# Graph layer on one core: 51 single-row fetch steps go from ScalarE's DMA queue to GpSimd's gathers

## The reference, cut to what matters

```
h    = relu(layernorm(x))
w    = edge_weight / segment_sum(edge_weight, dst)[dst]
feat = relu(h @ W_pool + b_pool)
neigh  = segment_max(feat[src] * w, dst)
rst  = h @ W1_self + neigh @ W1_neigh + b1;  h1 = relu(rst / |rst|)
neigh2 = segment_sum(h1[src] * w, dst) / deg
out  = x + relu(h1 @ W2_self + neigh2 @ W2_neigh + b2)
```

## Time and profile before

| | us |
|---|---|
| median of 3 runs | 5000.1 |
| lowest and highest | 4995.1, 5009.1 |
| the profiled execution | 5002.4 |
| its span in the trace | 5000.6 |

### The profile page before, as it was taken

The page is one execution under the profiler, slowest core; times in us unless marked ns, Lnnn a source line. Parts: engine busy times, 40 slices in busy tenths (PEclk is TensorE's granted clock), DMA queues, the critical chain, the costliest instruction groups (busy, mean ns, idle before and its releaser), DMA issues.

```text
span 5000.6 us, 64383 instructions
## 1 busy us (share of the span) xinstructions
PE 3637.2 (73%) x15531; PEld 1723.2 (34%) x15531; DVE 3011.2 (60%) x6735; ACT 1430.3 (29%) x4018; POOL 2954.1 (59%) x3127
## 2 busy tenths in 40 slices
PE   1345663588888888887557888888888888888864
PEld 1334442233333333333323333333333333333323
DVE  1656665566666666666446656666666666666654
ACT  1434443222222222222443222222222222222220
POOL 6366656655565555565656555655555555655655
PEclk5756565699999999998768999998999999999977
DMA  4244332322223222322433233232323333333236
GB/s 135 82 144 134 99 97 96 101 91 92 87 88 97 87 86 90 94 88 93 128 92 93 91 97 99 93 106 89 96 89 101 96 95 101 96 93 103 91 112 175
DMA packets 283743, 502.39 MB, mean 100 GB/s; under 512 B 64740, under 2 KB 200164, under 8 KB 258532
## 3 DMA queue, kind: packets, MB, share of 16 engines
q1 hardware_dynamic: 170756, 290.79, 16.8%
q0 software_dynamic: 99552, 204.13, 15.5%
q10 hardware_dynamic: 13056, 3.37, 0.3%
HBM read 260.17 MB, written 237.86 MB: 100 GB/s over the span
## 4 chain that ended last, share of the span: by engine, by line
ACTq 37%; issue 21%; PE 19%; ACT 6%; DVE 6%; another core or an unknown queue 6%; DVEq 3%; DMA 1%; POOL 1%; SPq 0%; POOLq 0%
ACTq L704 29%; ACTq L719 7%; PE pM L1250 3%; ACT pT L741 3%; PE pM L1248 3%; ACT pM L741 2%; PE pM L1249 2%; PE pC L1250 2%; PE pC L1248 2%; PE pC L1249 2%; DVEq L952 2%; DVE S L958 1%; DVE CP L1036 1%; DVE S L955 1%
## 5 line engine op out<-in xcount | busy, mean ns | idle before, releaser
L609 POOL DMA_INDIRECT G<-h_tab,SRC x1437 | 1359.0, 946 | 954.8 <-issue 429.5
L609 POOL DMA_INDIRECT G<-feat_tab,SRC x1390 | 1320.9, 950 | 943.6 <-issue 391.8
L1036 DVE TENSOR_SCALAR CP<-pH,kcode 128x1024 bf16<-128x1024 bf16 x1225 | 912.6, 745 | 352.1 <-PE pC L1250 115.7
L741 ACT ACTIVATE pM<-G,EW 128x128 f32<-128x128 f32 x1440 | 530.8, 371 | 1621.2 <-issue 1482.6
L741 ACT ACTIVATE pT<-G,EW 128x128 f32<-128x128 f32 x1387 | 509.0, 370 | 1302.1 <-issue 1139.7
L1036 DVE TENSOR_SCALAR U<-pR,kcode 128x1024 bf16<-128x1024 bf16 x735 | 547.3, 745 | 94.3 <-PE pM L1250 46.8
L1248 PE MATMUL pC<-CP,A 128*128 128x512 bf16 x1274 | 506.7, 398 | 125.0 <-DVE CP L1036 82.5
L1248 PE MATMUL pM<-CP,A 128*128 128x512 bf16 x1176 | 467.2, 397 | 129.0 <-DVE CP L1036 87.0
L1249 PE MATMUL pC<-CP,A 128*128 128x512 bf16 x1274 | 505.3, 397 | 18.7 <-issue 17.0
L955 DVE SCALAR_TENSOR_TENSOR S<-S,C,pM 128x128 f32<-128x128 f32 x780 | 271.2, 348 | 372.2 <-ACT pM L741 233.5
L1222 PE MATMUL pH<-CP 128*128 128x98 bf16 x1563 | 301.2, 359 | 266.6 <-DVE CP L974 133.7
(11 more groups left out here) (203 smaller groups left out, 4193.8 us busy)
## 6 DMA issues: line engine op xcount, KB each, us to landing
scan<-S SPq DMA_DIRECT2D x97, 1032.0 KB
scan<-S SPq DMA_DIRECT2D x97, 1024.0 KB
GA<-h_tab ACTq DMA_DIRECT2D x3328, 0.5 KB
GA<-feat_tab ACTq DMA_DIRECT2D x3200, 0.5 KB
G<-h_tab,SRC POOLq DMA_INDIRECT x1437
G<-feat_tab,SRC POOLq DMA_INDIRECT x1390
U<-own_tab SPq DMA_DIRECT2D x48, 256.0 KB
CP<-codes SPq DMA_DIRECT2D x25, 256.0 KB
```

Of the source, the lines that this page charges most:

```text
L609: pool.indirect_dma_start(out=dst, out_offset=None, in_=table, in_offset=bass.IndirectOffsetOnAxis(ap=idx, axis=0)).then_inc(s, 16)
L741: act.activation(scaled(t), v, ACT.Copy, scale=EW[:, t:t + 1]).then_inc(s_mul, 1)
L1036: dve.tensor_scalar(HOT[phase][:, k % NHOT, :], sources(phase).bitcast(BF16), kcode[:, j:j + 1], None, ALU.is_equal).then_inc(s_o2, 1)
```

## The change

ScalarE fetches no rows any more. The 51 steps of `ROWA` join `GORD`, in the order of their steps, so GpSimd makes 1415 gathers in phase 0 and 1463 in phase 1, through the same ring of 16 buffers. The buffers `GA`, the offsets `IX`, their load, their shift on VectorE and the waits for them go. All else is as before.

```diff
-ROWA = [(phase, row_step(phase, m)) for phase in range(2) for m in range((25, 26)[phase])]
-FETCHED = set(ROWA)
-GORD = [(0, t) for t in SEQ if (0, t) not in PAT and (0, t) not in FETCHED] + \
-    [(1, t) for t in range(TS) if (1, t) not in PAT and (1, t) not in FETCHED]
+GORD = [(0, t) for t in SEQ if (0, t) not in PAT] + [(1, t) for t in range(TS) if (1, t) not in PAT]
...
-        GA = sb("GA", [P, NGS, D])
-        IX = sb("IX", [P, P], I32)
...
-                    sp.dma_start(IX[:, :], srcr).then_inc(s_ixl, 16)
...
-            def fetch_row(to, phase, reg, s):
-                at = act.snap(reg, donate=True)
-                act.dma_start(to.bitcast(U8), flat[phase][bass.ds(at, 4 * D)].rearrange("(a d) -> a d", a=1))\
-                    .then_inc(s, 16)
...
-                    if p == 0 and k >= NGS:
-                        ph, before = ROWA[k - NGS]
-                        act.wait_ge(s_mul, ph * TS + before + 1)
-                    if p % RL == 0:
-                        ahead[:] = [act.alloc_register(f"arow{k}_{p + r}") for r in range(RL)]
-                        act.load(ahead, IX[k:k + 1, p:p + RL])
-                    fetch_row(GA[p:p + 1, k % NGS, :], phase, ahead[p % RL], s_arow[k % NGS])
...
-                fetch_rows(phase, t)
...
-                elif (phase, t) in AAT:
-                    k = AAT[phase, t]
-                    act.wait_ge(s_arow[k % NGS], 16 * P * (k // NGS + 1))
-                    v = GA[:, k % NGS, :]
...
-                    dve.wait_ge(s_ixl, 16)
-                    dve.tensor_scalar(IX[:, :], IX[:, :], 9, None, ALU.logical_shift_left).then_inc(s_ix, 1)
```

More of the change, by code:

```diff
@@ L123 @@
 TWO = 0x40000000
-U8 = mybir.dt.uint8
 def tiles_of(g):
@@ L165, in own_store_block, with build @@
     return (OWN_FIRST + OWN_EACH * (g + 1)) // T + 1
-def build(nc, x, src, srcq, srcr, dstx, ew, w_pool, b_pool, w1s, w1n, b1, w2s, w2n, b2, out):
+def build(nc, x, src, srcq, dstx, ew, w_pool, b_pool, w1s, w1n, b1, w2s, w2n, b2, out):
     feat = nc.dram_tensor("feat_tab", (NP, D), F32).ap()
@@ L328, in build @@
         s_sst = [sem(f"s_sst{i}") for i in range(NS)]
-        s_arow = [sem(f"s_arow{i}") for i in range(NGS)]
-        s_ixl = sem("s_ixl")
-        s_ix = sem("s_ix")
         s_oh = sem("s_oh")
@@ L460, in raw_arrived @@
                 eng.wait_ge(s_x[max(i for i in range(len(LOADS)) if sum(LOADS[:i]) <= g)], 16)
-        flat = [tab.rearrange("n d -> (n d)").bitcast(U8) for tab in (feat, htab)]
         block = ctx.enter_context(nc.Block())
@@ L697, in _ @@
                     act.activation(C[:, :], M[:, :], ACT.Identity, scale=-NEG, bias=neg[:, 0:1]).then_inc(s_c, 1)
-            ahead = []
-            def fetch_row(to, phase, reg, s):
-                at = act.snap(reg, donate=True)
-                act.dma_start(to.bitcast(U8), flat[phase][bass.ds(at, 4 * D)].rearrange("(a d) -> a d", a=1))\
-                    .then_inc(s, 16)
[L707 to L713, removed]
-                    if p == 0 and k >= NGS:
-                        ph, before = ROWA[k - NGS]
-                        act.wait_ge(s_mul, ph * TS + before + 1)
-                    if p % RL == 0:
-                        ahead[:] = [act.alloc_register(f"arow{k}_{p + r}") for r in range(RL)]
-                        act.load(ahead, IX[k:k + 1, p:p + RL])
-                    fetch_row(GA[p:p + 1, k % NGS, :], phase, ahead[p % RL], s_arow[k % NGS])
             def multiply(phase, t):
                 n = slot_of(phase, t)
-                fetch_rows(phase, t)
                 if (phase, t) in PAT:
@@ L759, in _ @@
             act.wait_ge(s_ew, 16)
-            act.wait_ge(s_ix, 1)
             act.wait_ge(s_h0, NGR)
@@ L1384, in _ @@
             node_stage(1, s_y)
-_NAMES = ["x", "src", "srcq", "srcr", "dstx", "ew", "w_pool", "b_pool", "w1s", "w1n", "b1", "w2s", "w2n", "b2"]
+_NAMES = ["x", "src", "srcq", "dstx", "ew", "w_pool", "b_pool", "w1s", "w1n", "b1", "w2s", "w2n", "b2"]
 def kernel(x, src, dst, edge_attr_128, edge_weight, L0_gnn_W_pool, L0_gnn_b_pool, L0_gnn_W1_self,
@@ L1406 @@
     srcq = np.stack([srcs[:, list(quad_steps(u))].T.reshape(-1) for u in range(QN)])
-    srcr = filled(np.stack([srcs[:, t] for _, t in ROWA]), 0, P, 0)
-    given = [filled(x, 0, NP, 0), srcs[:, order], srcq, srcr, dstx, filled(edge_weight, 0, EP, 0),
+    given = [filled(x, 0, NP, 0), srcs[:, order], srcq, dstx, filled(edge_weight, 0, EP, 0),
              L0_gnn_W_pool, L0_gnn_b_pool, L0_gnn_W1_self, L0_gnn_W1_neigh, L0_gnn_b1,
```

## The result

The changed kernel takes **5115.9 us** (median of 4 runs, 5105.7 to 5124.3); the kernel before took 5004.6 beside it. The ratio is 1.0226, 95% interval 1.0201 to 1.025: **slower by 111 us**, where 331 us of gain were forecast. The profiled execution has a span of 5114.6 us.

The account below looks back on a forecast made before the run. The prediction took ScalarE's queue, late with row fetches, as the bound. Savings of 125 (steps 0 to 567), 15 (first 52 steps) and 191 us (pick stages) made 331: 5002.4 - 331 = 4671 us, range 4330 to 4930.

Parts of the forecast that it names:

- 4.4% of the new length: Pick stages: TensorE's waits for VectorE fall to this share, as in the stretch without fetching, saving 191 us.
- Steps 0 to 567: Max phase before TensorE's picks, 742 us: 125 us saved, between 80 and 148.
- the next late engine is GpSimd: Steps 0 to 567: GpSimd's 480 gathers at 1.25 us, 600 us, set the pace once ScalarE is relieved.
- First 52 steps: Start of the sum phase, 98 us, with the splits: 15 us saved, between 0 and 33.
- Pick stages: Both phases' steps with picks on TensorE, 1378 and 2095 us: 191 us saved, between 0 and 329; TensorE is next engine.
- the other end is 0: Pick stages: the lowest gain allowed for was nothing, against 329 us if TensorE's waits for VectorE all went.
- Everything else that TensorE loses is its own: Pick stages: losses besides waits for VectorE are TensorE's late starts with no waker and the half clock after them.
- The row for it: Stretch without fetching after 4742 us: 51 steps took 77 us, 1.51 us per step against 1.47 with fetching.
- No change: Rival, 5000 us, chance 0.05: TensorE's late starts eat the early gain, the pick stages losing 140 of 3473 us.
- Held gathers: Rival, edge stages, 5130 us: VectorE's work holds gathers, 1.60 us each; chance 0.12 together with any other loss.
- three signs I named for being wrong: Gathers longer than 1.1 us; TensorE's late starts with no waker growing by more than 190 us; or those starts vanishing.
- 0.86 + 0.37 = 1.23 us per step for ScalarE: ScalarE's queue before the change, good stretches: 0.86 us per step for fetching 2.25 rows, beside a multiply of 0.37.

Follow-up runs that it names:

- e9: The changed kernel with no gathers in the edge stages, zeros multiplied in place of the gathered rows: 3820.7 us, ratio 0.7569 to the kernel before.
- e18: The kernel before with ScalarE fetching 2.75 rows per step in place of 2.25, on a fifth chip: 4264.7 us, where the kernel before took 3932.9 us.
- e12: The kernel before with its row fetches but no gathers in the edge stages, zeros multiplied instead: 3906.5 us, ratio 0.7811.
- e1: The kernel before without its row fetches and without gathers in their place, 51 steps multiplying zeros: 5091.4 us, ratio 1.011.
- e15: The changed kernel with two unused activations on ScalarE ahead of every multiply: 5254.4 us, ratio 1.0457 to the kernel before.
- e2: The kernel before with all its row fetches kept and the 51 gathers of the changed kernel added: 5114.7 us, ratio 1.0167.
- e7: The changed kernel with one gather in sixteen left out, zeros multiplied instead: 4934.5 us, ratio 0.9787 to the kernel before.
- e13: The changed kernel with each of its 2878 gathers fetching 64 rows in place of 128: 5152.7 us, ratio 1.0303 to the kernel before.
- e8: The changed kernel with four of the six matmuls of each pick left out: 4942.6 us, ratio 0.9803 to the kernel before.

## Why the prediction was wrong

**Right.** ScalarE left the chain; gathers were not held (943 ns); GpSimd did not become the late engine; SyncE's order did nothing. TensorE's waits with a waker fell by 168 us, where the working had 191 (its own rule, 4.4% of the new length, gives 184; it took 4.4% of the rest).

**Steps 0 to 567: 125 us forecast, 6 found.** The step that failed is "the next late engine is GpSimd", 1.25 us per gather, 617 us in all. The stage takes 736 us, and GpSimd waits 151 of them for multiplies. Without gathers (e9) it takes 503, and with gathers but no slow stretches at most 656 (e18, where ScalarE's longer queue is the bound). So some 80 to 120 us of the stage (736 against 656 and 617) can be put down to the slow stretches, which fall on all three other engines: instructions with no waker start 102 us late on ScalarE, 54 on VectorE and 101 on TensorE's matmuls.

**First 52 steps: 15 forecast, 7 found.** The right size.

**Pick stages: 191 gained in the forecast, 131 lost.** The failing step is "the other end is 0": the term was bounded at nothing from below, and the time that TensorE loses with no waker was taken as its own and constant ("Everything else that TensorE loses is its own"). It rose by 171 us, and the lower clock took 84. The row for it stood in the prediction: 1.51 us per step in the 77 us without fetching, against 1.47. I set it aside as short and used its wait share instead. The changed kernel runs the same steps at 1441 / 936 = 1.54 and 2163 / 1424 = 1.52 us per step.

**The rivals.** "No change" named the mechanism, late starts that eat the gain, with a chance of 0.05 and a price of 140 us; it was worth more than the whole gain. "Held gathers" (5130) came within 15 us of the measured time by luck: no gather was held. Of the three signs I named for being wrong, the second came true in kind: the late starts grew, by 171 us where I had put the bound at 190.

**What lay behind it.** I read the 4.20 us for two row issues as ScalarE's own slowness. The same 0.70 us spacing stood on TensorE in the same trace: of its 68 groups of two or more such starts (under 5 us apart) 56 lie within 1 us of a group of ScalarE's, where shifting them by 30 to 93 us leaves 27. A delay that several engines share moved to the next one when ScalarE was relieved. The working's 0.86 + 0.37 = 1.23 us per step for ScalarE was too long besides: e12, with the same 2.25 rows, runs the sum phase's pick stage at 1649 / 1510 = 1.09.

**Open.** Removing the fetches alone costs 1.1% (e1), and ScalarE's occupancy is not the reason (e15). A gather more or less moved the time by 1.65 us (e2) and 1.17 to 1.31 us (e7), though all gathers together cost 1340 / 2878 = 0.47 us each. Both prices lie near 4587 / 2878 = 1.59 us, the changed kernel's edge stages per gather, as if a run of gathers and the stop behind it set the pace (theory D); that is argued, and no run tests it. Nor does any run say what in a gather brings the stretches, its instruction or its packets, or why one chip has none. Fewer, larger gathers, and runs cut short by a pause on GpSimd, would be the next things to try. No version that does all the work beat the kernel before.

## What to carry to other kernels

When an engine's queue is late with nothing to wait for, look at the other engines' starts at the same microseconds: if they are spaced alike, relieving one engine may only move the delay. A short stretch of the old trace that already runs like the new kernel deserves weight: here its pace (1.51 us per step) was nearer the result than the sum of parts. Before a quarter of the time is put down to one cause, ask what else the experiment took away. And time a pair of kernels on more than one chip where such stretches are in the trace, since the bound can be another one.

## What the runs showed of the hardware

- Slow stretches: TensorE, ScalarE and SyncE start an instruction only every 0.70 us, for some 3 to 8 us at a time, and VectorE is slowed too. The kernel before takes 5004 to 5050 us on four chips that show them and 3933 on a fifth that does not (e18). They need gathers (e9, e12) and do not go by rows or bytes (e13: 64 rows in place of 128, as many packets). In the changed kernel 89 of 98 begin at the 11th to 16th gather without a pause.
- TensorE's clock was granted at 0.96 to 1.00 in the pick stages without slow stretches (e9, e12, e18), at 0.92 and 0.94 in the kernel before and at 0.88 after the change; behind such a stretch, at 3010.72 in the changed kernel, a matmul took 0.63 us, not 0.38.
- The Trainium skill ("Runtime: NRT & Kernel Launch", section "Instruction fetch mechanics") says that instruction fetch is hidden behind the rate of dispatch. The instruction queue of TensorE moved the same 122 packets, 2.00 MB, with 273 late starts as with 679 or 6, and half of that, 61 packets, with 693 (e8). A packet took a median of 1.08, 1.01 and 0.99 us in the first three, and 1.06 in e18. So neither the amount fetched nor the time of a packet explains them; whether a fetch is asked for late, no run here shows.
- Beside 1225 picks of 0.745 us a gather of the sum phase was not longer than alone, in every kernel that gathers 128 rows (means of 943 to 946 ns, against 0.95 us alone in the earlier trace rows); the hold by the scan in the earlier trace rows has no counterpart there.
